# The last attention's first batch begun inside the latent experts' last batch

## The reference

```python
# layer 2, feed-forward: latent experts
h = x @ down_w + down_b                       # 256 -> 128
logits = x @ router_w + router_b - COST_LAMBDA * cost
probs = softmax(logits); topv, topi = top_k(probs, 2); gate = softmax(topv)
for k in range(2):
    mask = one_hot(topi[..., k], 8)
    for e, (w1, b1, w2, b2) in enumerate(expert_params):
        hm = h * mask[..., e:e + 1]
        acc = acc + (gelu(gelu(hm) @ w1 + b1) @ w2 + b2)
    out = out + acc * gate[..., k:k + 1]
out = out + 0.1 * (gelu(gelu(h) @ shared_w1 + shared_b1) @ shared_w2 + shared_b2)
out = out @ up_w + up_b
out = out + (gelu(x) @ core_w + core_b)
# layer 3, attention: norm, q, k, v of 16 heads of 16 by Wqkv, softmax(q k^T / 4) v, Wproj, bproj
```

## Time and profile before

| what | value |
|---|---|
| median of 3 runs | 1832.93 us (1827.65 to 1840.35) |
| the profiled execution | 1827.52 us, span 1825.7 us |
| PE busy | 1608.8 us, 88% of the span |
| DVE, ACT, POOL busy | 62%, 48%, 26% |
| mean granted TensorE clock | 0.947 of full speed |

### The profile page before, as it was taken

The page is one execution under the profiler, slowest core; times in us unless marked ns, Lnnn a source line. Parts: engine busy times, 40 slices in busy tenths (PEclk is TensorE's granted clock), DMA queues, the critical chain, the costliest instruction groups (busy, mean ns, idle before and its releaser), DMA issues. The chain is left out here.

```text
span 1825.7 us, 28978 instructions
## 1 busy us (share of the span) xinstructions
PE 1608.8 (88%) x10726; PEld 963.0 (53%) x10726; DVE 1134.3 (62%) x2567; ACT 867.9 (48%) x1361; POOL 469.0 (26%) x596
## 2 busy tenths in 40 slices
PE   5899999799989999952999999689999999998776
PEld 2344444388866666541556665367764444443533
DVE  2787787333446666468577776355545788774475
ACT  1256565533325555532155555457761666665322
POOL 4222210033322330010333220036762522300000
PEclk9999999999989999965999999879999999999698
DMA  7452350200235424000643560211206435320322
GB/s 248 107 128 65 81 145 1 95 0 0 77 91 162 133 80 114 1 10 27 178 116 83 128 162 2 87 45 54 80 25 174 112 80 145 115 48 13 112 94 93
DMA packets 68962, 160.30 MB, mean 88 GB/s; under 512 B 10286, under 2 KB 15927, under 8 KB 67963
## 3 DMA queue, kind: packets, MB, share of 16 engines
q1 hardware_dynamic: 68826, 158.51, 30.6%
HBM read 109.05 MB, written 53.09 MB: 89 GB/s over the span
## 5 line engine op out<-in xcount | busy, mean ns | idle before, releaser
L1165 DVE TENSOR_REDUCE a_mx<-PS 128x1 f32<-128x512 f32 (+3 forms) x768 | 392.3, 551 | 188.1 <-PE PS L1425 128.1
L1362 ACT ACTIVATE a_pT<-PS 128x1024 f32<-128x1024 f32 (+3 forms) x384 | 310.2, 811 | 228.1 <-PE PS L1451 159.2
L1420 PE MATMUL PS<-a_k,a_q 64*128 64x512 f32 (+3 forms) x768 | 233.9, 415 | 16.7 <-DVE a_mx L1165 13.6
L440 DVE CUSTOM_DVE_ANT_0 PS<-PS,a_dist 128x448 f32<-128x448 f32 x256 | 156.1, 643 | 51.1 <-PE PS L685 48.7
L1442 PE MATMUL PS<-a_q,a_k 64*128 64x512 f32 (+3 forms) x768 | 174.0, 437 | 7.2 <-PEq L98 2.0
L1465 PE MATMUL PS<-a_pT,a_va 128*32 128x512 f32 (+3 forms) x1536 | 164.5, 500 | 3.1 <-ACT a_raw L1315 2.9
L590 ACT ACTIVATE a_pT<-PS 128x448 f32<-128x448 f32 (+1 forms) x256 | 124.6, 541 | 84.6 <-PE PS L708 84.2
L1442 PEld LDWEIGHTS PS<-a_q,a_k 64*128 64x128 f32 x768 | 76.0, 185 | 144.9 <-issue 70.5
L1420 PEld LDWEIGHTS PS<-a_k,a_q 64*128 64x128 f32 x768 | 109.0, 187 | 69.9 <-DVE a_mx L1165 57.0
L157 PE MATMUL PS<-cst 128*128 128x512 f32 x192 | 102.9, 667 | 36.7 <-PEq L98 28.6
L2361 POOL TENSOR_TENSOR f_h_low<-f_prod,f_h_high 128x512 fp32r<-128x512 f32 x84 | 109.9, 1315 | 60.4 <-ACT f_h_high L2548 57.6
(11 more groups left out here) (362 smaller groups left out, 3436.6 us busy)
## 6 DMA issues: line engine op xcount, KB each, us to landing
spread_scratch<-a_high SPq DMA_DIRECT2D x96, 256.0 KB, 3.0
a_q<-spread_scratch SPq DMA_DIRECT2D x96, 256.0 KB, 5.5
a_k<-spread_scratch SPq DMA_DIRECT2D x96, 256.0 KB, 6.2
f_gb<-gate_rows SPq DMA_DIRECT2D x68, 256.0 KB, 5.2
spread_scratch<-a_low SPq DMA_DIRECT2D x48, 256.0 KB, 4.0
a_q<-window_scratch SPq DMA_DIRECT2D x32, 256.0 KB, 5.6
a_k<-window_scratch SPq DMA_DIRECT2D x32, 256.0 KB, 6.4
window_scratch<-a_high SPq DMA_DIRECT2D x24, 256.0 KB, 4.7
```

The costliest lines, as they stand in the source:

```text
L440: dve.tensor_tensor_reduce(PS[:, 4 + a, 0:KW], PS[:, 4 + a, 0:KW], dt_[:, off:off + KW], 1.0, 3e38, ALU.add, ALU.min, mx[:, gg % 2, qt, 2 ...
L1165: dve.tensor_reduce(mx[:, gg % 2, qt, 2 * half + a:2 * half + a + 1], PS[:, tile_bank(t), 0:kw], AX.X, ALU.max).then_inc(max_done, 1)
L1362: act.activation(pT[:, N // 2 % 2, N % 2, :, q0:S], PS[:, 2 * (N % 2):2 * (N % 2) + 2, q0:S], ACT.Exp, scale=SCALE).then_inc(exp_done, 1)
L1420: mm = pe.matmul(ps[:, 0:kw], q[b % 2][rows, pair, qt * P:(qt + 1) * P], k[b % 2][rows, pair, 0:kw], start=True, stop=not causal)
```

## The change

The front of a3 moves into the last batch of the latent experts, as a1's does in swiglu. PE makes the two turns behind unit 0 of that batch, the projected units behind 2, 4 and 5, and the value pieces behind 7 and 10. DVE takes the norm's statistics and application behind units 15 and 18 of the batch before, the weights' and the input's low parts behind 20, 0 and 1, and the norm of the next batch behind 8 and 11. The 24 score tiles stand behind the last projection, with two banks in turn, and the experts' last output pieces between the twelfth and the thirteenth. The fillers of that front are gone. Behind the barrier stay groups 2 and 3 of the spread (in a1 too, where they were fetched ahead of it), the output weights, the bias, the memsets of the second halves, and Y = X + bias. Tiles of q, k, values and m are cut in halves so that they fit into freed places, and the input weights land where their low parts are made.

```diff
@@ attention_quads, SP
-            def spread_batch(b):
+            def spread_first(b):
                 store_unit(b, 0)
                 store_unit(b, 1)
                 fetch_group(b, 0)
                 fetch_group(b, 1)
                 store_unit(b, 2)
                 store_unit(b, 3)
+
+            def spread_last(b):
                 fetch_group(b, 2)
                 fetch_group(b, 3)
 
             def loop():
+                if bias is not None:
+                    sp.dma_start(bb[:, :], bias.rearrange("(a n) -> a n", a=1).broadcast_to([P, D])
+                                 ).then_inc(loaded_bias, 16)
+                spread_last(0)
+                load_last()
                 for b in range(1, NB):
-                    spread_batch(b)
+                    spread_first(b)
+                    spread_last(b)
...
@@ attention_quads, POOL
             def fill_rest():
+                pool.memset(m[1][:, :, :], 0.0).then_inc(preset, 1)
                 pool.memset(zeros[:, :], 0.0).then_inc(preset, 1)
-                pool.memset(va[1][:, :, :, :], 1.0).then_inc(preset, 1)
-                pool.wait_ge(preset, 6)
+                for half in va[1]:
+                    pool.memset(half[:, :, :, :], 1.0).then_inc(preset, 1)
+                pool.wait_ge(preset, 9)
...
@@ latent_experts, SP, POOL
+                following = ahead.sync(sp)
+                following.load()
+                following.spread_first(0)
...
+                    if b == NB - 2 and n == 16:
+                        following.norm()
+                    if b == NB - 1 and n == 6:
+                        following.fill()
+                    if b == NB - 1 and n == 7:
+                        following.norm_next()
+                following.split_maxima(0)
...
@@ latent_experts, DVE
+                    if n == 0:
+                        following.weights_low(1)
+                    elif n == 1:
+                        following.input_low()
+                    elif n in (4, 5, 6, 7):
+                        following.keep_unit(n - 4)
+                    elif n == 8:
+                        following.norm_stats(1)
+                    elif n == 11:
+                        following.norm_apply(1)
...
+                    if b == NB - 2 and n == 15:
+                        following.norm_stats(0)
+                    if b == NB - 2 and n == 18:
+                        following.norm_apply(0)
+                    if b == NB - 2 and n == 20:
+                        following.weights_low(0)
+                    if b == NB - 1:
+                        follow_up(n)
+                for t in range(12):
+                    following.maxima(t)
                 for i in range(TB // 2):
                     add_outputs(NB - 1, i)
+                for t in range(12, 20):
+                    following.maxima(t)
+                following.keep_maxima(0, 0)
+                for t in range(20, 24):
+                    following.maxima(t)
...
@@ latent_experts, PE
+                    if n == 0:
+                        pe.wait_ge(lat_kept, NB)
+                        pe.wait_ge(gT_kept, NB)
+                        pe.wait_ge(o_added, TB // 2 * (NB - 2))
+                        following.turn(0, 0, host.turn_banks[0])
+                        following.turn(0, 1, host.turn_banks[1])
+                    elif n == 2:
+                        following.unit(0)
+                        following.unit(1)
+                    elif n == 4:
+                        following.unit(2)
+                    elif n == 5:
+                        pe.wait_ge(y_kept, NB - 1)
+                        following.unit(3)
+                        pe.wait_ge(ahead.unit_low[1], 1)
+                    elif n == 7:
+                        following.values(0)
+                        pe.wait_ge(ahead.unit_low[2], 1)
+                    elif n == 9:
+                        pe.wait_ge(ahead.va_done, 1)
+                        pe.wait_ge(ahead.unit_low[3], 1)
+                    elif n == 10:
+                        pe.wait_ge(o_added, TB // 2 * (NB - 2) + 1)
+                        following.values(1)
...
-                for i in range(TB // 2):
-                    outputs(NB - 1, i)
+                        if b == NB - 1:
+                            follow_up(n)
+                for t in range(12):
+                    following.scores(t)
+                pe.wait_ge(ahead.va_done, TB // 2)
+                outputs(NB - 1, 0)
+                outputs(NB - 1, 1)
+                for t in range(12, 20):
+                    following.scores(t)
                 pe.wait_ge(o_added, TB // 2 * NB)
...
+                following.turn_maxima(0, 0)
+                for t in range(20, 24):
+                    following.scores(t)
+    return ahead
...
@@ build
+                    start = ground.at("w1_high")
+                    Y = nc.alloc_sbuf_tensor_at("Y", [P, NT, D], F32, offset=start)
```

More of the change, by code:

```diff
@@ L66, in take, with again, at @@
         size += -size % 32
-        span = next(s for s in self.free if s[1] - s[0] >= size)
-        self.taken[name] = (span[0], span[0] + size)
-        span[0] += size
+        if name in self.fixed:
+            self.taken[name] = (self.fixed[name], self.fixed[name] + size)
+        else:
+            span = next(s for s in self.free if s[1] - s[0] >= size)
+            self.taken[name] = (span[0], span[0] + size)
+            span[0] += size
         return self.nc.alloc_sbuf_tensor_at(f"{self.tag}_{name}", shape, dt, offset=self.taken[name][0])
+    def again(self, name, shape, dt=F32):
+        return self.nc.alloc_sbuf_tensor_at(f"{self.tag}_{name}_in", shape, dt, offset=self.taken[name][0])
+    def at(self, name):
+        return self.taken[name][0]
     def outside(self, spans):
@@ L98, in stage_semaphores, with layer_norm_buffers @@
     nc.all_engine_barrier()
[L101 removed]
+def layer_norm_buffers(ctx, nc, tag, sem, tiles=TB, take=None):
     def sb(name, shape):
@@ L1441, in scores_T @@
                     rows = slice(64 * a, 64 * a + 64)
-                    mm = pe.matmul(PS[:, 2 * half + a, q0:S], k[b % 2][rows, pair, kt * P:(kt + 1) * P],
-                                   q[b % 2][rows, pair, q0:S], start=True, stop=not causal)
+                    mm = pe.matmul(PS[:, 2 * half + a, q0:S], k[b % 2][g // 2][rows, pair, kt * P:(kt + 1) * P],
+                                   q[b % 2][g // 2][rows, pair, q0:S], start=True, stop=not causal)
                 if causal:
@@ L2624, in latent @@
                     for c in range(KC):
-                        mm = pe.matmul(PS[:, 5, :], down[:, c, :], xnT[:, c, b * S:(b + 1) * S], start=(c == 0),
+                        mm = pe.matmul(PS[:, 5, :], down[:, c, :], xnT[b][:, c, :], start=(c == 0),
                                        stop=(c == KC - 1))
```

269 lines of the change are left out of this document (154 added, 115 removed).

## The result

The changed kernel takes 1838.32 us (median of 20 runs, 1833.3 to 1850.15), the kernel before 1832.31 us (median of 20, 1823.9 to 1840.35). The ratio is 1.0036, 95% interval 1.0020 to 1.0052: 6 us slower. A second measurement later gave 1.0027 (1.0008 to 1.0047). The forecast was a gain of 4 us; the time lies inside its range and on the other side of no change.

The account below looks back on a forecast made before the run. PE was taken as full in the latent experts' last batch and the last attention's loop, with 54.1 us between them to attack. 18.4 - 9.1 - 4 - 1.2 = 4.1 us gained; 1832.9 - 4.1 = 1829 us, range 1815 to 1840.

Parts of the forecast that it names:

- Stalls in the batch: Latent experts' last batch: PE waits for moved work queued on DVE, ACT and POOL; 2.7 us lost, bounds 0 and 7.
- moved PE work: Latent experts' last batch: transposes, units and value pieces moved onto full PE lengthen it by 9.5 us.
- third rival: Last batch: DVE and POOL get in each other's way, stall 7 instead of 2.7, gain 0, 1833 us; chance 0.15.
- The tail: From the last projection to the last attention's loop: score tiles, outputs, maxima, keeping and boundary take 23.5 us.
- fourth rival: Tail: clock falls at the first tiles, outputs take 10.8 instead of 5.4, 9 us together; slower, 1838 us; chance 0.15.
- POOL's chain: Last attention's loop start: memsets, bias, Y, then splits delay PE's turn to 20.0 us behind the begin; 9.1 us lost.
- The clock behind it: Last attention's loop, after PE's wait for POOL: about 8 us of work at half rate, 4 us lost, between 0 and 8.
- The second attention: Second attention: group 2, now fetched behind the boundary, lands after its first score was due; 1.2 us lost, bounds 0 and 3.
- gain of 18.4 us at the loop's begin: Last attention's loop begins at 1402.0 instead of 1420.36, before losses behind it: 18.4 us gained.

Follow-up runs that it names:

- run 1: Changed kernel with the load of a3's weights on SyncE issued ahead of the wait for the last batch's gates; ratio to before 0.9972, 1828.3 us.
- run 6: Changed kernel with the four normalizations of a3's second batch moved from behind unit 11 to behind score tile 11; ratio to before 1.0007, 1835.8 us.
- run 3: Changed kernel with a filler matmul behind every second score tile of the tail, 12 in all; ratio to before 1.0036, 1839.0 us.
- run 4: Changed kernel with the last batch's two output steps halved and laid behind score tiles 5, 7, 9 and 11; ratio to before 1.0023, 1836.6 us.
- Run 2: Changed kernel with GpSimd's 16 additions of input and bias moved behind the split of the second group's maxima; ratio to before 0.9993, 1832.0 us.
- 7: Changed kernel with GpSimd's three memsets placed singly behind units 3, 4 and 5 instead of together behind unit 6; ratio to before 1.0016, 1839.2 us.
- kernel 9: kernel 8 plus filler matmuls behind score tiles 13, 15, 17, 21 and 23; ratio to before 0.9950, 1820.4 us.
- kernel 5: Changed kernel with the edits of run 1, Run 2 and run 4 together; ratio to before 0.9949, 1824.4 us.
- kernel 8: Changed kernel with the edits of run 1, Run 2, run 4 and 7, plus a third score-tile bank; ratio 0.9903, 1814.7 us; repeated 0.9915, 1819.6 us.

## Why the prediction was wrong

The trace lost 8.2 us of span where 4.1 of gain were summed. The 12.3 between them, by the prediction's own terms:

- **Stalls in the batch, 2.7 (bounds 0 and 7): this step failed.** The stretch grew by 24.4, of which 9.5 is the moved PE work, so the stalls were 14.9. Half of them, 7.3 us, is the weights' load, which run 1 removed. I followed the queues of PE, DVE, ACT and POOL unit by unit and costed SP's part by its stores and fetches "some 35 us earlier"; where the weights' load stands on SP I never asked. It is behind the wait for the last batch's gate rows, so that it was issued at 1322.61, 0.3 us after its first reader wanted it; a transfer that was hidden in before became the last thing to arrive. What is left, 7.6, is near the third rival's price of 7. PE's waits in kernel 1 say where it lies: they sum to 8.1 us, against 1.5 in before, and 4.3 of them are those for VectorE in the fence above, 0.9 the one for the memsets, 2.7 seven short ones for low parts (in before four, 1.5), 0.2 one for an addition to X. That GpSimd lengthens VectorE's instructions is shown by run 6, and 1.2 us of PE's waits go with it there; that the other waits for VectorE have this cause too, and not only the moved work that stands ahead in its queue, is not shown. The Trainium skill's page "SBUF — State Buffer", section "SBUF: two separate sides", has a rule for it: VectorE, in its two-port modes or with two sources in SBUF, and GpSimd share a port pair that is locked for a whole instruction. The trace agrees: 4.43 us against 1.37, and the weight difference at 2.34 against 1.23, while products with one operand in PSUM kept their 0.69. In which mode the normalizations ran no run shows.
- **The tail, 23.5: short by 5.2.** Term by term: the first twelve tiles to the end of their maxima 9.3 instead of 8.3; from there to the thirteenth maximum, with the outputs between, 7.75 instead of 5.1; the other twelve maxima and the keeping 10.0 instead of 9.0; the boundary 1.7 instead of 1.2. The fourth rival's mechanism came true at its place, the first tiles, and the outputs took 7.9 us, not its 10.8. Its pointer against itself, that PE held its clock near 1740 with less to do, misled me. But the clock is only half of it: run 3 held it at 1.00, made the outputs 2.6 us shorter and won 0.2 in all, run 4 won 5.2 by giving VectorE work while the outputs ran. That the median came out at this rival's 1838 is partly chance, since it had no late weights.
- **POOL's chain, 9.1: right.** 20.2 us against 20.0 predicted, in the order and with the durations given (bias 0.88 us of wait, since the memsets cover most of its 3.3; additions 11.02). Run 2 confirms the cause. Its own worth is 6.8 of the 9.3.
- **The clock behind it, 4: too large.** It was 0.50 from 1440 to 1444 and 0.85 to 1448, but from the second to the third group's turn went 17.1 us (16.7 to 17.3 in the other kernels that leave POOL's chain alone) against 16.3 in before: 0.4 to 1.1 us. Why half the clock cost so little stays open; no run bears on it.
- **The second attention, 1.2: not borne out.** Group 2's first tile stands 10.8 us behind the loop's begin in after (545.05 behind 534.29), and at 10.7 in before; the row at 539.33 that I took for it was a tile of the group before. So nobody waited for the later fetch. Later in the same stretch after is 1.3 us behind, at the first turn of maxima in the loop, 17.8 us against 16.5, and the clock there was 0.50 in 544 to 548, where before had 0.76. But the changed kernel again, and kernels 6 and 7, have the same 16.5 as before, and all thirteen executions with this code go from 12.4 to 18.0. So no cost of the change is seen, and that 1.2 looked right in the first trace was chance. PE of after, and of the changed kernel again, whose loop begins at 538.12:

```profile
545.05 0.77 PE L1439 MATMUL PS<-a_k0b,a_q0b 64*128 64x512 f32 x2
...
552.07 0.66 PE L1492 MATMUL PS<-cst,a_m 128*128 128x128 f32 x4
```

```profile
554.58 0.66 PE L1492 MATMUL PS<-cst,a_m 128*128 128x128 f32 x4
```

The sum: 17.4 us later at the loop's begin than predicted (12.2 by stalls, 5.2 by the tail), 5.2 less lost behind it than the 14.3 of the last three terms. The gain of 18.4 us at the loop's begin was really 0.9. So the forecast missed the direction by the stalls and the tail, and two losses put too high, the clock's and the second attention's, made the miss smaller than it would have been.

## What to carry to other kernels

When a stage's front moves into the end of the stage before, its loads move too. Write down for each where its queue stands and how long it takes to land, ahead of its first reader, and put loads without a dependence ahead of the first wait on that queue. Work that was free on an idle engine is not free when it is pushed over a boundary; place it behind what that engine owes the critical path. Where PE only feeds VectorE, keep VectorE fed by cutting PE's long pieces and laying them between; filler matmuls (runs 3 and 9) held the clock and cost what they brought.

## What the runs showed of the hardware

Four VectorE normalizations (one source and the result in SBUF) took 4.43 us beside GpSimd's subtractions and 1.37 alone, 4.43 to 4.45 in every execution that has them there. Those of the first batch took 3.28 to 3.29 in every kernel with the weights early, beside two subtractions, and 1.38 to 1.39 in the others traced, where GpSimd was idle. Beside the 4.43 us GpSimd paid nothing, its subtractions took their usual 1.3 each; beside VectorE's weight difference, which reads two sources in SBUF, both paid: 2.34 us instead of 1.23, and GpSimd's next subtraction, begun at 1335.10, took 2.26.

The granted clock is not a fixed property of the code. With the outputs in halves the first of them ran at 1.00 in kernel 4 and at 0.62 in kernel 5 with the same instructions in the tail, and the tails differ by 1.6 us. In the second attention the way from the loop's begin to the first turn of maxima took 18.0 us in one execution of kernel 8 and 12.5 in the other: the clock was 0.50 for 12 us (536 to 548) in the first, and in the second 0.65 over 4 us (544 to 548) and 1.00 behind them. From one block to the next PE idled 1.7 to 2.7 us, and in kernel 9, with fillers right up to that gap, the clock fell to 0.50 all the same, some 4 us behind the last of them.
